# The last two steps of an encoder and the start of an attention: class tokens inverted and split on their own, last reciprocal and product moved

## The reference

```python
def _ln(x, g, b):
    m = x.mean(-1, keepdims=True)
    v = ((x - m) ** 2).mean(-1, keepdims=True)
    return (x - m) * lax.rsqrt(v + EPS) * g + b

def _expert(x, p):
    h = _ln(jax.nn.relu(x @ ew1 + eb1) @ ew2 + eb2, eg, ebeta)
    qkv = h @ aiw + aib
    q, k, v = jnp.split(qkv, 3, axis=-1)
    q, k, v = (heads(q), heads(k), heads(v))
    attn = jax.nn.softmax(jnp.einsum('bhqd,bhkd->bhqk', q, k) * SCALE, axis=-1)
    o = jnp.einsum('bhqk,bhkd->bhqd', attn, v).transpose(0, 2, 1, 3).reshape(h.shape)
    h = o @ aow + aob
    ...
```

## Time and profile before

| | |
|---|---|
| median of 3 runs | 3918.48 us (3917.52 to 3924.34) |
| profiled execution | 3914.89 us, of which span 3913.2 us |
| PE busy | 3557.7 us, 91% |
| DVE busy | 2630.0 us, 67% |
| ACT busy | 2154.0 us, 55% |
| POOL busy | 1246.7 us, 32% |
| mean granted TensorE clock | 0.958 of full speed |

### The profile page before, as it was taken

How to read it: one execution, slowest core, us unless ns; L and a number is a source line. 1 busy time by engine, 2 the same in 40 slices (tenths; PEclk the granted TensorE clock), 3 DMA queues, 4 the chain that set the end, 5 groups by cost and what they waited for, 6 DMA issues and landing times. The chain is left out here.

```text
span 3913.2 us, 94499 instructions
## 1 busy us (share of the span) xinstructions
PE 3557.7 (91%) x35332; PEld 2160.7 (55%) x35332; DVE 2630.0 (67%) x4691; ACT 2154.0 (55%) x4252; POOL 1246.7 (32%) x1112
## 2 busy tenths in 40 slices
PE   6868789889889899899999999999999949999997
PEld 5654356556556556345555555555555436676665
DVE  7866678778678678756666666666666654555555
ACT  6857468668568578544444444444444455555554
POOL 0026478578478478310000000000000004444443
PEclk8889899999989999999999999999999969999999
DMA  9930100100100110421111211111121131211121
GB/s 174 177 60 2 59 17 0 45 17 0 45 17 0 45 66 0 152 81 46 46 50 44 51 46 50 47 45 49 46 51 46 41 119 50 57 50 44 55 57 32
DMA packets 391038, 203.24 MB, mean 52 GB/s; under 512 B 150861, under 2 KB 385106, under 8 KB 390234
## 3 DMA queue, kind: packets, MB, share of 16 engines
q1 hardware_dynamic: 390482, 201.03, 20.5%
q10 hardware_dynamic: 392, 0.03, 0.0%
HBM read 143.48 MB, written 57.51 MB: 51 GB/s over the span
## 5 line engine op out<-in xcount | busy, mean ns | idle before, releaser
L201 POOL MEMSET h_ident<- 128x128 f32 x1 | 0.2, 204 | 1444.3 <-POOLq L81 1444.3
L1888 ACT ACTIVATE l_gates<-l_gates 128x768 f32<-128x768 f32 x260 | 219.2, 843 | 349.2 <-DVE l_gates L1832 349.1
L1832 DVE SCALAR_TENSOR_TENSOR l_gates<-banks,l_unscale,l_bias 128x1024 f32<-128x1024 f32 x260 | 333.8, 1284 | 99.8 <-PE banks L1658 98.4
L1658 PE MATMUL banks<-l_w,l_xs 128*64 128x512 f16 x3120 | 362.0, 382 | 7.5 <-DVE l_xs L1745 6.6
L1658 PE MATMUL banks<-plot,l_xs 128*64 128x512 f16 x3120 | 359.9, 380 | 0.0
L2185 PE MATMUL banks<-h_mem,h_w 128*128 128x320 f16 x2496 | 357.7, 300 | 0.0
L1658 PE MATMUL banks<-l_w,out_t 128*64 128x512 f16 x3072 | 352.9, 379 | 1.7 <-DVE out_t L1751 1.7
L1658 PE MATMUL banks<-plot,out_t 128*64 128x512 f16 x3072 | 352.8, 379 | 0.0
L667 POOL TENSOR_TENSOR ax_p<-ax_p,ax_ri 128x520 f32<-128x520 f32 (+1 forms) x256 | 284.8, 1113 | 163.7 <-DVE ax_ri L887 163.5
L2480 ACT ACTIVATE h_work<-banks,h_bias,h_factor 128x320 f32<-128x320 f32 x312 | 192.3, 616 | 261.1 <-PE banks L2185 257.2
L1892 ACT ACTIVATE l_ig<-l_kept 128x256 f32<-128x256 f32 x260 | 108.3, 417 | 354.2 <-DVE l_kept L1849 352.2
(11 more groups left out here) (386 smaller groups left out, 7318.0 us busy)
## 6 DMA issues: line engine op xcount, KB each, us to landing
out_t<-x_scratch SPq DMA_DIRECT2D x130, 256.0 KB, 3.0
mem_scratch<-out_t SPq DMA_DIRECT2D x520, 64.0 KB, 2.0
h_mem<-mem_scratch SPq DMA_DIRECT2D x104, 320.0 KB, 3.6
image<-in_x_dram SPq DMA_DIRECT2D x132, 196.0 KB
x_scratch<-plot SPq DMA_DIRECT2D x4, 4160.0 KB, 16.4
ring<-in_x_dram SPq DMA_DIRECT2D x60, 196.0 KB
plot<-in_L_ffn_attn_in_w_dram SPq DMA_DIRECT2D x4, 768.0 KB, 4.5
h_scratch<-plot SPq DMA_DIRECT2D x1, 2080.0 KB, 6.5
```

Source lines behind the costliest of these rows:

```text
L1658: mm = pe.matmul(ps[d * HALF:(d + 1) * HALF, 2 * z + n, :], lhsT, w_of[e][:, d, kk, b, n * 512:(n + 1) * 512], start=(kk == 0 and turn_ == ...
L1832: dve.scalar_tensor_tensor(out=gz.rearrange("p (n c) -> p n c", n=2), in0=ps[:, 2 * z:2 * z + 2, :], scalar=unscale[:, e:e + 1], in1=bias[ ...
L1888: act.activation(gates[:, z, 0:3 * D], gates[:, z, 0:3 * D], ACT.Sigmoid).then_inc(gated, 1)
```

## The change

The last normalizations get an order of their own.
- Steps 8 and 9 hold the class tokens of images 52 to 57 and 58 to 63 (`CLASSES`). `class_late` inverts just those columns of `sd` and multiplies just those columns of `hc`, on VectorE, into `class_h`; `class_early` copies the 52 others from `h` once step 7's product has ended; `class_split` splits `class_h` instead of `h`. `dve_first` is not called in the experts any more, and VectorE's wait for all of `h_ready` is gone.
- The last reciprocal (step 9) goes behind the class split and the clearing of the banks, ahead of the wait for `first_kept` (`rest` in `dve_run`). The last product goes behind the first class mask on GpSimd (`rest` in `pool_run`), followed by a wait for its own signal.
- At k = 9 VectorE inverts step 7 before it splits unit 0, instead of after. The subtraction for unit 1 goes from after k = 11 to the end of k = 10.
- `pe_begin` and unit 0's `act_keys` go from after k = 11 to after k = 10.
- Step 9's halves are not added on GpSimd: its variance is two matmuls that accumulate, one per half.

```diff
-    def pool_run(self, pool, e, src):
+    def pool_run(self, pool, e, src, rest=None):
         mask_keys(base, 0, 0, base * GROUP)
         pool.wait_ge(self.first_kept, BASE + 2 * e + 1)
         mask_class(0, base * GROUP)
+        if rest is not None:
+            rest()
         self.run(pool, e, unit_)
...
-        self.dve_first(dve, e, src)
+        if rest is None:
+            self.dve_first(dve, e, src)
         for lo, hi in ((0, 1), (2 * SEQ - 1, 2 * SEQ + 1), (4 * SEQ - 1, 4 * SEQ + 1)):
             dve.memset(ps[:, 0:4, lo:hi], 0.0).then_inc(self.cleared, 1)
+        if rest is not None:
+            rest()
         dve.wait_ge(self.first_kept, BASE + 2 * e + 1)
...
+        LATE = 2
+        CLASSES = [-(-(WSTEPS - LATE + i) * WIDE // SEQ) for i in range(LATE)] + [IMAGES]
...
-                    if live(1):
+                    if live(1) and k < WSTEPS:
                         pool.wait_ge(squared, BASE + e * STEPS + k)
                         pool.tensor_tensor(sq[:, 1 - par, 0], sq[:, 1 - par, 0], sq[:, 1 - par, 1], ALU.add).then_inc(halved, 1)
-                    if live(2):
+                    if live(2) and k < WSTEPS + 1:
+                        normalize(k - 2)
...
+                def last_tokens():
+
+                    normalize(WSTEPS - 1)
+                    pool.wait_ge(h_ready, BASE + (e + 1) * STEPS)
...
-                att.pool_run(pool, e, h)
+                att.pool_run(pool, e, h, last_tokens)
...
+                    if k == WSTEPS + 1:
+                        pe.wait_ge(squared, BASE + (e + 1) * STEPS)
+                        pe.wait_ge(rooted, BASE + at - 2)
+                        for kk in range(KD):
+                            mm = pe.matmul(ps[:, 4, 0:WIDE], mean[:, :], sq[:, par, kk, :], start=(kk == 0), stop=(kk == KD - 1))
+                        mm.then_inc(varied, 1)
-                laid_steps(body, {0: sum_vectors, 1: sum_betas, 3: sum_values, 4: turn_most, 5: share_most, WSTEPS + 1: begin})
+                laid_steps(body, {0: sum_vectors, 1: sum_betas, 3: sum_values, 4: turn_most, 5: share_most, WSTEPS: begin})
...
+                def class_late(i):
+
+                    j, some = WSTEPS - LATE + i, slice(CLASSES[i], CLASSES[i + 1])
+                    columns = slice(CLASSES[i] * SEQ - j * WIDE, WIDE, SEQ)
+                    n = CLASSES[i + 1] - CLASSES[i]
+                    dve.wait_ge(rooted, BASE + e * STEPS + j + 1)
+                    dve.reciprocal(class_inv[:, some], sd[:, j % 2, columns]).then_inc(class_inverted, 1)
+                    dve.wait_ge(class_inverted, BASE + e * LATE + i + 1)
+                    dve.tensor_tensor(class_h[:, :, some], hc[:, j % RING, :, columns],
+                                      class_inv[:, some].unsqueeze(1).broadcast_to([P, KD, n]), ALU.mult).then_inc(class_ready, 1)
+
+                def class_early():
+
+                    dve.wait_ge(h_ready, BASE + e * STEPS + WSTEPS - LATE)
+                    first = h[:, :, :].rearrange("p c (b t) -> p c b t", t=SEQ)[:, :, 0:CLASSES[0], 0]
+                    dve.tensor_copy(class_h[:, :, 0:CLASSES[0]], first).then_inc(class_ready, 1)
+
+                def class_split():
+
+                    dve.wait_ge(class_ready, BASE + (e + 1) * (LATE + 1))
+                    dve.tensor_scalar(att.x0[:, 0], class_h[:, :, :], NORMED, None, ALU.mult).then_inc(class_high, 1)
+                    dve.wait_ge(class_high, BASE + e + 1)
+                    dve.scalar_tensor_tensor(out=att.x0[:, 1], in0=class_h[:, :, :], scalar=NORMED, in1=att.x0[:, 0],
+                                             op0=ALU.mult, op1=ALU.subtract).then_inc(att.x0_low, 1)
+
+                def invert(k):
+
+                    j = k - 2
+                    dve.wait_ge(rooted, BASE + e * STEPS + j + 1)
+                    if j >= 2:
+                        dve.wait_ge(h_ready, BASE + e * STEPS + j - 1)
+                    dve.reciprocal(rs[:, j % 2, :], sd[:, j % 2, :]).then_inc(inverted, 1)
...
-                    if live(2):
-                        dve.wait_ge(rooted, BASE + at - 1)
-                        if live(4):
-                            dve.wait_ge(h_ready, BASE + at - 3)
-                        dve.reciprocal(rs[:, par, :], sd[:, par, :]).then_inc(inverted, 1)
+                    if live(2) and k < WSTEPS:
+                        invert(k)
+                    if k == WSTEPS - 1:
+                        att.dve_split(dve, h, e * att.UNITS, 0, 0, e * att.UNITS * GROUP)
+                    if k == WSTEPS:
+                        class_late(0)
+                        class_early()
+                        invert(k)
+                        begin_second()
+                    if k == WSTEPS + 1:
+                        class_late(1)
+                        class_split()
                 laid_steps(body, {})
-                begin_second()
-                dve.wait_ge(h_ready, BASE + (e + 1) * STEPS)
-
-                att.dve_run(dve, e, ps, h, factor[:, 0:1])
+                att.dve_run(dve, e, ps, h, factor[:, 0:1], lambda: invert(WSTEPS + 1))
```

More of the change, by code:

```diff
@@ L858, in dve_first, with dve_run @@
                                  op0=ALU.mult, op1=ALU.subtract).then_inc(self.x0_low, 1)
-    def dve_run(self, dve, e, ps, src, factor):
+    def dve_run(self, dve, e, ps, src, factor, rest=None):
         base = e * self.UNITS
@@ L1296, in body @@
                             mm.then_inc(h2_done, 1)
-                    if live(2):
-                        pe.wait_ge(halved, BASE + at - 1)
+                    if live(2) and k < WSTEPS + 1:
+                        pe.wait_ge(halved, BASE + e * (STEPS - 1) + k - 1)
                         pe.wait_ge(rooted, BASE + at - 2)
                         pe.matmul(ps[:, 4, 0:WIDE], mean[:, :], sq[:, par, 0, :], start=True, stop=True).then_inc(varied, 1)
-                laid_steps(body, {0: sum_vectors, 1: sum_betas, 3: sum_values, 4: turn_most, 5: share_most, WSTEPS + 1: begin})
+                    if k == WSTEPS + 1:
[5 more added lines that the diff above has]
+                laid_steps(body, {0: sum_vectors, 1: sum_betas, 3: sum_values, 4: turn_most, 5: share_most, WSTEPS: begin})
                 att.pe_run(pe, e, ps, w_in, ident)
@@ L1452, in _ @@
                 laid_steps(body, {5: raise_weights, 9: begin_first,
[L1453 removed]
+                                  WSTEPS: lambda: att.act_keys(act, ps[:, 6, :], factor[:, 0:1], e * att.UNITS, 0)})
                 act.wait_ge(saved, BASE + e * 16)
```

17 lines of the change are left out of this document (9 added, 8 removed).

## The result

The changed kernel takes 3902.42 us (median of 5 runs, 3898.55 to 3907.89) against 3918.48 us (5 runs, 3915.69 to 3924.34): ratio 0.9955, 95% interval 0.9943 to 0.9968, so 16 us faster. The profiled execution has a span of 3906.2 us; in it the first encoder began 8 us later than in the one of before (its first matmul of the second linear at 457.3 instead of 448.9 us), ahead of all that the change touches. So spans are not compared here. I measure each boundary from the end of step 9's second matmuls instead, which is 1363.84 in the rows of before and 1360.71 in those of after. From the first to the last boundary, one expert took 287.9 us before and 283.6 after; the prediction had named 287.8 and 283.4.

A forecast was written before the change was run, and what follows sets the result against it. The bound was the single chain from the encoder's last step to the first scores, not the busiest engine. 4 x 4.45 = 17.8 us off the profiled 3914.9 gives 3897.1; with 3.6 us for the median, 3900.7; range 3890 to 3909.

The forecast's parts named there:

- what the fill keeps: Start of attention: unit 1's split ends 4.45 us earlier per boundary, and the fill keeps all of it.
- Split ahead of its wait: VectorE at step 9: inverting step 7 before splitting unit 0 covers a 1.56 us wait; gain on this path 1.95 us.
- Keys, queries and variance at the high clock: TensorE before step 9's root: 24 matmuls take 2.98 us and four variance passes 1.6 us at granted clock 1.00.
- The first rival: TensorE stays at the low clock over the two blocks: 12.8 us gained in all, 3905.7 us; chance 0.12.
- the halving's removal: Step 9's variance without GpSimd's halving addition: it waits for TensorE anyway, running 1367.5 to 1369.1.
- Class tokens of step 8: VectorE before step 8's inversion: early class work ends at 1366.2; costs nothing if under 0.25 us late.
- The hold: Step 9's class tokens: VectorE's small product and first split half stand still until GpSimd's own operation ends; split done at 1373.0.
- The second rival: Small VectorE operations pass GpSimd unheld: 26.6 us gained in all, 3891.9 us; chance 0.13.
- The moved reciprocal and product: Behind the class split: queries follow the reciprocal, class scores start at 1376.8 against 1381.65, gain 4.85 us.
- The third rival: Moved inversion and product bind queries and masks: 1.7 us a boundary stays, 6.8 in all, 3911.7 us; chance 0.10.
- The slower rival: Units after the fill collide on the lock: 33.3 us lost over 64 units, 3934 us; chance 0.05.

The follow-up runs named there:

- e3: Changed kernel with the old order at k = 9: unit 0's split first, step 7's inversion after it; 3908.6 us, 0.9966 of the kernel before.
- e2: Changed kernel with step 9's squares halved on GpSimd again and one variance matmul; 3899.2 us, 0.9943 of the kernel before.
- e1: Changed kernel with the two class buffers in a free part of a PSUM bank instead of SBUF; 3890.66 us, 0.9924 of the kernel before.
- e11: Kernel before, with 17, 10 and 7 extra matmuls in TensorE's three boundary gaps, nothing of the change; 3917.3 us, 0.9988 of the kernel before.
- e5: Changed kernel with 13 and 7 extra matmuls, results unread, behind step 9's variance and the class projections; 3892.04 us, 0.9922 of the kernel before.
- e4: Changed kernel with last reciprocal right behind the class split and last product back in the encoder, ahead of the key masks; 3910.2 us, 0.9968 of before.
- e7: Class buffers in PSUM, last reciprocal behind VectorE's first queries, last product behind unit 1's class mask on GpSimd; 3893.7 us, 0.9929 of the kernel before.
- e9: Changed kernel without the class path and the moved reciprocal and product; order, earlier keys and queries, two-matmul variance stay; 3914.0 us, 0.9978 of before.
- e10: Class buffers in PSUM, TensorE kept busy, reciprocal behind first queries, last product waiting for unit 1's split; 3888.10 us, 0.9923 of the kernel before.

## Why the prediction was right, step by step

The forecast was 3900.7 us, the result 3902.4. The mechanism and nearly all of its terms were right. The last term, what the fill keeps, was mis-sized twice, and the total came out so near because the two errors partly cancel, which is luck.

- **Split ahead of its wait.** Forecast: step 9 kept 1.2 us behind its matmuls; measured 1361.85 - 1360.71 = 1.14. e3 shows that this step alone is worth 2.3 us at the class scores, a little more than the 1.95 of the prediction's layout.
- **Keys, queries and variance at the high clock.** Forecast 2.98 and 1.6 us, measured 2.78 and 1.56, granted clock 1.00; root at 5.9 forecast, 5.4 measured. The first rival (low clock in these two blocks) did not happen. That the halving's removal is free was implied by the layout, and e2 shows it.
- **Class tokens of step 8.** The inversion behind them began 2.04 us after the reference point, forecast 2.4; as said, at no cost.
- **The hold.** Forecast 1.4 and 1.2 us for two tiny operations; measured 1.53 and 1.02, and e1 makes it a cause. The class split ended at 8.5, forecast 9.2; 0.5 of the difference is the earlier root. The second rival (small operations pass) gave 26.6 us, and e1, which makes them pass, gives 3918.5 x (1 - 0.9924) = 29.8.
- **The moved reciprocal and product.** Class scores at 13.0 forecast, 12.3 measured; VectorE's queries behind the reciprocal ended at 1372.55 and the class mask at 1372.63, and TensorE began at 1373.02. In every run but e11 the class scores started 0.44 to 0.47 us behind the queries or 0.10 to 0.12 behind the mask, whichever was later; here it is the queries. TensorE's list has the wait for the queries first and four more behind it, which may be the 0.4 us but was not tried. In e5 the mask ended 0.5 us earlier and the scores started no earlier, so the queries, as forecast, were what TensorE waited for. e4 shows what the move is worth. The third rival (moved work binds, 6.8 us in all) did not happen, though some of it is there: by these two distances the mask alone would have let TensorE begin 0.3 us sooner, and in e1, where the class split ends 2.0 us earlier, e7 shows that 0.9 us of the path was the reciprocal.
- **What the fill keeps.** This is the step that was mis-sized. I took 4.45 us from unit 1's split. The split itself came 22.56 - 17.51 = 5.05 us earlier on the mean of the four, and the attention ended 226.6 - 222.9 = 3.7 us earlier, 14.9 in all; in the second profile of the changed kernel it was 4.2, or 16.8. So the split gained 0.6 more than said, and 0.9 to 1.4 us was lost behind it. Of this, 0.8 in the first profile lies between the split and the third maximum (4.3 us on the mean, 3.5 before): unit 1's keys ran at the low clock in every expert (2.74 us), while before they had run at the high one in two experts of four. I had given the clock a place only ahead of the class split. Another 0.35 is the small loss of the next item. The time from boundary to boundary still came out as forecast, 283.6 us, because the encoders between were 0.4 us shorter than before on the mean, which is within their spread.
- **The slower rival.** No collisions settled in: from the 21st to the 64th maximum the kernels before and after agree within 0.1 us (135.91 before, 135.90 after in the first expert). One small loss remains open. Between the ninth and the 13th maximum all kernels with the class path take 13.0 us, and before, e9 and e11 take 12.6. It lies in one place of VectorE's list, between a maximum and its difference:

```profile
1400.47 0.83 DVE L873 TENSOR_REDUCE ax_mx<-banks 128x10 f32<-128x650 f32 x1 [0.68 <-PE banks L756]
1401.85 0.84 DVE L878 TENSOR_TENSOR ax_p<-banks,ax_mx 128x650 f32<-128x650 f32 x1 [0.54 <-DVE ax_mx L873]
```

The usual idle time between these two is 0.19 us. It is worth 4 x 0.35 = 1.4 us in all, and its cause was not found.

## What to carry to other kernels

When an engine's small operation comes out of a long chain, look at what its neighbour on a shared port will be doing at the new time: here 12 columns waited 1.3 us for a product, and a free part of a PSUM bank as their buffer took the wait away. Taking work out of a chain is worth only what the next one in the queue lets through; class tokens alone gave 0.7 us, and 2.9 once the product had left the queue too. And lay out TensorE's idle gaps beside a new schedule, not only its work: a gap moved earlier can put the low clock under matmuls that ran at the high one.

## What the runs showed of the hardware that I had not expected

The low clock cost the changed kernel 3.1 us an expert at the end of the attention, though TensorE had idle time to spare there: with extra matmuls in two gaps of 3.9 and 2.3 us the keys of unit 1 took 1.48 us instead of 2.74 in three experts of four, and the kernel 10 us less. In e10 an idle time of 2.1 us was followed by a low stretch of 3.4 us at all four boundaries. An operation of VectorE on PSUM ran beside GpSimd's in 0.18 us where the same one on SBUF took 1.53. And who starts first is decided by a few tenths: GpSimd 0.31 us ahead turned a split of 1.03 us into one of 2.19 (e7), and VectorE 0.17 us ahead took 0.75 us and made GpSimd's mask last 1.51 instead of 1.06 (e5).
